# A selective scan in one TensorE-heavy kernel: decay factors written into PSUM, u made in place, and a new order of the work

## What is computed

```python
x = silu(conv(x) + conv_b)                    # (B, 512, 512 channels)
dt = softplus(dt_low @ W_dt + b_dt)
A = -exp(A_log)                               # 512 channels x 16 states
h = exp(dt_t[..., None] * A) * h + (dt_t * x_t)[..., None] * B_t[:, None, :]
y_t = sum over states of h * C_t
y = (y + x * D) * silu(z)
```

## Time and profile before

| what | value |
|---|---|
| median of 3 runs | 4347.93 us (4346.42 to 4351.42) |
| profiled execution: its time | 4355.29 us |
| its span, first to last instruction | 4353.5 us |
| TensorE / VectorE / ScalarE / GpSimd busy | 3935.7 / 3872.0 / 2366.9 / 1724.7 us |
| mean granted clock of TensorE | 0.968 of full speed |
| DMA engines | 73.7% busy, 753.5 MB |

### The profile page before, as it was taken

How to read it: one execution, slowest core, us unless ns; L and a number is a source line. 1 busy time by engine, 2 the same in 40 slices (tenths; PEclk the granted TensorE clock), 3 DMA queues, 4 the chain that set the end, 5 groups by cost and what they waited for, 6 DMA issues and landing times.

```text
span 4353.5 us, 55576 instructions
## 1 busy us (share of the span) xinstructions
PE 3935.7 (90%) x18933; PEld 2043.7 (47%) x18933; DVE 3872.0 (89%) x5708; ACT 2366.9 (54%) x4341; POOL 1724.7 (40%) x1295
## 2 busy tenths in 40 slices
PE   5878889999999999999999999998989999998898
PEld 3333444444545445454544545454444545544555
DVE  7699989898998989899898989989899899998753
ACT  2444455656555565555556465565545656564544
POOL 1254434443434435353343444444344344433410
PEclk9989999999999999899999999999899999999999
DMA  2699787878778787876787777788786888878511
GB/s 64 160 209 219 173 210 167 203 161 191 181 166 202 177 202 166 185 192 160 184 188 188 178 178 189 164 209 174 167 199 140 207 171 218 177 183 190 135 55 42
DMA packets 241440, 753.50 MB, mean 173 GB/s; under 512 B 37650, under 2 KB 132659, under 8 KB 171524
## 3 DMA queue, kind: packets, MB, share of 16 engines
q1 hardware_dynamic: 241156, 749.95, 73.7%
HBM read 647.30 MB, written 101.71 MB: 172 GB/s over the span
## 4 chain that ended last, share of the span: by engine, by line
DVE 40%; PE 33%; DMA 10%; issue 9%; ACT 6%; POOL 1%; SPq 1%; DVEq 0%; ACTq 0%; POOLq 0%
DVE state L1767 11%; DVE mt L1846 6%; DVE u L1762 4%; PE m L1249 4%; DMA state<-dtx_scratch 3%; PE m L1276 3%; PE pd L1477 2%; DMA decay<-dt_scratch 2%; PE y L1350 2%; DMA gz_scratch<-front 2%; DVE front L1701 2%; PE y L1338 2%; DVE front L1672 2%; DVE front L1676 2%; DVE front L1578 1%
## 5 line engine op out<-in xcount | busy, mean ns | idle before, releaser
L824 POOL TENSOR_TENSOR state<-state,bc 128x1024 f32<-128x1024 f32 x512 | 1270.4, 2482 | 1305.8 <-DVE u L1762 1287.1
L1767 DVE TENSOR_TENSOR_SCAN state<-decay,u 128x1024 f32<-128x1024 f32 x512 | 1166.8, 2279 | 6.4 <-ACT decay L1050 1.7
L1050 ACT ACTIVATE decay<-decay,a_neg 128x511 f32<-128x511 f32 x1024 | 674.9, 713 | 168.3 <-DMA decay<-dt_scratch 167.6
L1249 PE MATMUL m<-w_gu,hats_m 128*128 128x480 f32 x1472 | 680.5, 582 | 67.1 <-DVE front L1676 44.5
L1762 DVE TENSOR_TENSOR u<-state,bc 128x1024 f32<-128x1024 f32 x512 | 640.8, 1252 | 45.1 <-DMA state<-dtx_scratch 36.4
L1249 PEld LDWEIGHTS m<-w_gu,hats_m 128*128 128x128 f32 x1472 | 255.4, 192 | 334.5 <-issue 154.6
L805 POOL TENSOR_TENSOR front<-front,hsc_m 128x704 f32<-128x704 f32 x128 | 199.3, 1557 | 509.3 <-DVE front L1581 509.3
L1276 PE MATMUL m<-w_dn,front 128*128 128x256 f32 x1476 | 366.4, 390 | 14.1 <-ACT front L983 13.2
L1196 PE MATMUL y<-minus,zero 128*128 128x512 bf16 x1292 | 341.8, 389 | 2.1 <-ACT vec L904 2.1
L1338 PE MATMUL y<-state,sel 128*32 128x512 f32 x2048 | 280.6, 621 | 47.6 <-POOL state L824 47.3
L1276 PEld LDWEIGHTS m<-w_dn,front 128*128 128x128 f32 x1476 | 270.1, 191 | 103.8 <-ACT front L983 48.8
(11 more groups left out here) (396 smaller groups left out, 7278.3 us busy)
## 6 DMA issues: line engine op xcount, KB each, us to landing
decay<-dt_scratch SPq DMA_DIRECT2D x256, 1024.0 KB, 7.4
state<-dtx_scratch SPq DMA_DIRECT2D x256, 1024.0 KB, 11.5
qk_scratch_main<-shared SPq DMA_DIRECT2D x60, 384.0 KB, 4.3
shared<-qk_scratch_main SPq DMA_DIRECT2D x360, 64.0 KB
kh<-qk_scratch_main SPq DMA_DIRECT2D x360, 64.0 KB
xs_scratch<-front SPq DMA_DIRECT2D x16, 1024.0 KB, 9.5
dt_scratch<-front SPq DMA_DIRECT2D x256, 64.0 KB, 2.7
dtx_scratch<-hats_m SPq DMA_DIRECT2D x256, 64.0 KB, 5.0
```

The lines of the kernel that those rows point to most:

```text
L824: eng.tensor_tensor(st, st, bc[:, 1:2, :].to_broadcast([P, WIDE, L]), ALU.mult).then_inc(scan_pool.sem, scan_pool.step(f"c{r}{h}"))
L1050: ins = eng.activation(d, d, ACT.Exp, scale=a_neg[:, g:g + 1])
L1249: mm = eng.matmul(f.bank(r, f"gu{t}{p}")[:, 0:2 * width], norm.hat_t[:, k, t * P:(t + 1) * P], w_gu[:, k, 2 * lo:2 * (lo + width)], start= ...
L1767: eng.tensor_tensor_scan(st, decay[:, n % ND, h * WIDE * L:(h + 1) * WIDE * L], u[:, :], 0.0, ALU.mult, ALU.add).then_inc(scan_dve.sem, sc ...
```

## The change

The exponentials now go from the decay slot into a PSUM tensor `powers` of 1024 columns, the former `u`; its column 0 of both banks is set to 0 once by two one-column copies, and the 64 memsets of `dt` are gone. Each pair of exponentials waits for the scan before it. u is computed in place in the state's slot, one operation of 2048 columns a round, and the scan reads `powers` and the state and writes the state. The decay slot is free for the next load when its last exponentials are done. GpSimd's first product of a round waits for the first scan, its second for the next round's u. All five strings of `ORDER` are new. Two places of `ORDER` (the begin of VectorE's string), and then the rest, without the renaming of `u` to `powers` in a memset:

```diff
@@ -78,168 +78,165 @@
...
     "DVE":
-        "33333333333333330000000000000000000000000000000000000000000000000000333333333333333330000000000000000333333300000000000110000000"
...
+        "33333333333333330000000000000000000000000000000000000000000000000000333333333333333333300000000000000003333300000000000000010100"
...
@@ -366,12 +363,12 @@
-        u = ctx.enter_context(nc.psum_tensor("u", [P, WIDE * L], F32))
+        powers = ctx.enter_context(nc.psum_tensor("powers", [P, WIDE * L], F32))
-        U = [u[:, 0:L], u[:, L:2 * L]]
+        U = [powers[:, 0:L], powers[:, L:2 * L]]
@@ -503,11 +500,11 @@
         head_act = Steps(sem("head_act"), ["x0", "x1"] + [f"{n}{m}" for n, m in CONVS] + ["pj"]
                          + [f"{n}{c}" for b in (0, 2) for part in (("abs", "exp", "one"), ("ln",)) for c in (b, b + 1) for n in part] + [f"tanhz{m}" for m in range(C)])
         head_dve = Steps(sem("head_dve"), [n for w, m in CONVS for n in ((f"tap{m}1", f"tap{m}2", f"tap{m}3") if w == "conv" else (f"silu{m}",))]
-                         + [f"{n}{c}" for c in range(C) for n in ("rest", "log", "dt", "dtx", "zero")] + [f"siluz{m}" for m in range(C)])
+                         + [f"{n}{c}" for c in range(C) for n in ("rest", "log", "dt", "dtx")] + [f"siluz{m}" for m in range(C)])
         scan_pe = Steps(sem("scan_pe"), [n for r in range(ROUNDS) for n in ([f"skip{r // Q}"] if r % Q == 0 else []) + [f"sum{r}"]] + [f"o{t}" for t in range(T)])
         scan_act = Steps(sem("scan_act"), [f"decay{r}{h}" for r in range(ROUNDS) for h in range(PARTS)] + ["res0", "res1"])
         scan_dve = Steps(sem("scan_dve"), [n for r in range(ROUNDS)
-                                           for n in ([f"gate{r // Q - 1}"] if r >= Q and r % Q == 1 else []) + [f"{n}{r}{h}" for h in range(PARTS) for n in ("u", "scan")]]
+                                           for n in ([f"gate{r // Q - 1}"] if r >= Q and r % Q == 1 else []) + [f"u{r}"] + [f"scan{r}{h}" for h in range(PARTS)]]
                          + [f"gate{C - 1}"])
         scan_pool = Steps(sem("scan_pool"), [f"c{r}{h}" for r in range(ROUNDS) for h in range(PARTS)])
         CONVW = lambda tap, c: vec[:, tap * C + c:tap * C + c + 1]
@@ -643,7 +640,7 @@
                 eng.wait_ge(head_act.sem, head_act.after(i, "pj"))
                 eng.dma_start(bc_scratch[i], pj[RK + 1:, :]).then_inc(bc_saved, 16)
                 for c in range(C):
-                    for name, src, dst, done in (("zero", dt, dt_scratch, dt_saved), ("dtx", dtx_of(i), dtx_scratch, dtx_saved)):
+                    for name, src, dst, done in (("dtx", dt, dt_scratch, dt_saved), ("dtx", dtx_of(i), dtx_scratch, dtx_saved)):
                         for j in range(Q):
                             yield
                             if j == 0:
@@ -666,7 +663,7 @@
 
                 def load_bc(w):
                     if i and w == 0:
-                        eng.wait_ge(scan_dve.sem, scan_dve.after(i - 1, f"u{ROUNDS - 1}{PARTS - 1}"))
+                        eng.wait_ge(scan_dve.sem, scan_dve.after(i - 1, f"u{ROUNDS - 1}"))
                     if i and w == 1:
                         eng.wait_ge(scan_pool.sem, scan_pool.after(i - 1, f"c{ROUNDS - 1}{PARTS - 1}"))
                     eng.wait_ge(bc_saved, 16 * (i + 1))
@@ -683,7 +680,7 @@
                     n, c = ROUNDS * i + r, r // Q
                     yield
                     if n >= ND:
-                        eng.wait_ge(scan_dve.sem, scan_dve.after((n - ND) // ROUNDS, f"scan{(n - ND) % ROUNDS}{PARTS - 1}"))
+                        eng.wait_ge(scan_act.sem, scan_act.after((n - ND) // ROUNDS, f"decay{(n - ND) % ROUNDS}{PARTS - 1}"))
                     if r % Q == 0:
                         eng.wait_ge(dt_saved[c % 2], 64 * (2 * i + c // 2 + 1))
                         eng.wait_ge(dtx_saved[c % 2], 64 * (2 * i + c // 2 + 1))
@@ -819,8 +816,8 @@
                         st = state[:, n % NU, h * WIDE * L:(h + 1) * WIDE * L].rearrange("p (j l) -> p j l", j=WIDE)
                         if r == 0 and h == 0:
                             eng.wait_ge(bc_loaded[1], 16 * (i + 1))
-                        m = r * PARTS + h + 1
-                        eng.wait_ge(scan_dve.sem, scan_dve.after(i, f"u{m // PARTS}{m % PARTS}" if m < ROUNDS * PARTS else f"scan{r}{h}"))
+                        behind = h == PARTS - 1 and r < ROUNDS - 1
+                        eng.wait_ge(scan_dve.sem, scan_dve.after(i, f"u{r + 1}" if behind else f"scan{r}{h}"))
                         eng.tensor_tensor(st, st, bc[:, 1:2, :].to_broadcast([P, WIDE, L]), ALU.mult
                                           ).then_inc(scan_pool.sem, scan_pool.step(f"c{r}{h}"))
 
@@ -1045,9 +1042,14 @@
                         yield
                         if j == 0:
                             eng.wait_ge(decay_loaded[n % ND], 16 * (n // ND + 1))
-                        d = decay[:, n % ND, j * L + 1:(j + 1) * L]
+                        if n == 0 and j == 0:
+                            for bank in U:
+                                eng.activation(bank[:, 0:1], zero16[:, 0:1], ACT.Copy)
+                        if (n or j) and j % WIDE == 0:
+                            m = n * PARTS + j // WIDE - 1
+                            eng.wait_ge(scan_dve.sem, scan_dve.after(m // PARTS // ROUNDS, f"scan{m // PARTS % ROUNDS}{m % PARTS}"))
                         g = (r // Q * Q + j) * Q + r % Q
-                        ins = eng.activation(d, d, ACT.Exp, scale=a_neg[:, g:g + 1])
+                        ins = eng.activation(U[j % WIDE][:, 1:L], decay[:, n % ND, j * L + 1:(j + 1) * L], ACT.Exp, scale=a_neg[:, g:g + 1])
                         if j % WIDE == WIDE - 1:
                             ins.then_inc(scan_act.sem, scan_act.step(f"decay{r}{j // WIDE}"))
                 for b in range(2):
@@ -1725,9 +1727,6 @@
                     if c >= 2:
                         eng.wait_ge(dtx_saved[b], 64 * (2 * i + 1))
                     eng.tensor_tensor(dtx_of(i)[:, b, :], dt[:, b, :], xs[:, c, :], ALU.mult).then_inc(head_dve.sem, head_dve.step(f"dtx{c}"))
-                    yield
-                    eng.wait_ge(head_dve.sem, head_dve.after(i, f"dtx{c}"))
-                    eng.memset(dt[:, b, 0:1], 0.0).then_inc(head_dve.sem, head_dve.step(f"zero{c}"))
                 for m in range(C):
                     yield
                     eng.wait_ge(head_act.sem, head_act.after(i, f"tanhz{m}"))
@@ -1749,22 +1748,19 @@
                     if r >= Q and r % Q == 1:
                         yield
                         finish(r // Q - 1)
+                    yield
+                    if r == 0:
+                        eng.wait_ge(bc_loaded[0], 16 * (i + 1))
+                    eng.wait_ge(state_loaded[n % NU], 16 * (n // NU + 1))
+                    rows = state[:, n % NU, :].rearrange("p (j l) -> p j l", j=Q)
+                    eng.tensor_tensor(rows, rows, bc[:, 0:1, :].to_broadcast([P, Q, L]), ALU.mult).then_inc(scan_dve.sem, scan_dve.step(f"u{r}"))
                     for h in range(PARTS):
                         yield
                         st = state[:, n % NU, h * WIDE * L:(h + 1) * WIDE * L]
                         if h == 0:
-                            if r == 0:
-                                eng.wait_ge(bc_loaded[0], 16 * (i + 1))
-                            eng.wait_ge(state_loaded[n % NU], 16 * (n // NU + 1))
-                        if n or h:
-                            m = (n * PARTS + h - 1) // PARTS
-                            eng.wait_ge(scan_dve.sem, scan_dve.after(m // ROUNDS, f"scan{m % ROUNDS}{(h - 1) % PARTS}"))
-                        eng.tensor_tensor(u[:, :].rearrange("p (j l) -> p j l", j=WIDE), st.rearrange("p (j l) -> p j l", j=WIDE),
-                                          bc[:, 0:1, :].to_broadcast([P, WIDE, L]), ALU.mult).then_inc(scan_dve.sem, scan_dve.step(f"u{r}{h}"))
-                        yield
-                        eng.wait_ge(scan_dve.sem, scan_dve.after(i, f"u{r}{h}"))
+                            eng.wait_ge(scan_dve.sem, scan_dve.after(i, f"u{r}"))
                         eng.wait_ge(scan_act.sem, scan_act.after(i, f"decay{r}{h}"))
-                        eng.tensor_tensor_scan(st, decay[:, n % ND, h * WIDE * L:(h + 1) * WIDE * L], u[:, :], 0.0, ALU.mult, ALU.add
+                        eng.tensor_tensor_scan(st, powers[:, :], st, 0.0, ALU.mult, ALU.add
                                                ).then_inc(scan_dve.sem, scan_dve.step(f"scan{r}{h}"))
                 yield
                 finish(C - 1)
```

309 lines of the change are left out of this document (153 added, 156 removed).

## The result

| | before | changed |
|---|---|---|
| median | 4347.18 us (4 runs) | **4388.92 us** (4387.04 to 4392.70, 4 runs) |
| ratio, 95% interval | | 1.010 [1.0078, 1.0122] |
| profiled execution: time, span | 4355.29, 4353.5 us | 4387.04, 4384.9 us |

The change makes the kernel 41.7 us slower. The forecast was 4330, on the other side of no change.

The account below looks back on a forecast made before the run. VectorE was taken to bound the kernel, having the least slack. Terms -47 - 4 + 24 + 9 + 10 - 10 = -18 from the profiled 4355.3 us gave 4337.3, less 7.4 4330 us; range 4283 to 4393.

Parts of the forecast that it names:

- the term for GpSimd's C products, +10 us: VectorE operations with two SBUF inputs held while GpSimd's earlier-released product runs: +10 us, bounds 0 and 96.
- the added 96 us: Products' remaining time at VectorE's two-SBUF-input operations, 291 us before and 387 after; a tenth was taken as paid.
- u, -47: On VectorE, 512 operations of 1024 columns become 256 of 2048: -47 us, bounds 15 and 73 of gain.
- busy down by 50 to 60 us: Sign that the forecast is right: VectorE's busy time in the profile after falls by 50 to 60 us.
- Handing over the exponentials, +24 and +9: VectorE's scans waiting for ScalarE's exponentials: +24 us in 88 short first-to-second gaps, +9 us in the other 168.
- The decay slot, -10: Slot freed when its exponentials are done, so SyncE's loads go out earlier and u waits less: -10 us, bounds 0 and -36.
- The memsets, -4: The 64 memsets of column 0, 59 ns each, are dropped: -4 us.
- the case without loss: Rival "no handover loss": short gaps lie where VectorE was idle anyway; -61 us, 4287 us, chance 0.09.
- the exponentials' rival: VectorE waits before scans for exponentials, ScalarE working in order: +43, 4391 us, chance 0.26; decides from 51 us of waiting.
- The mean of L1727 far over 794: Sign of the port rival: VectorE's L1727 with a mean far over its 794 ns in the profile after.
- absorbed: Rival of no change: TensorE, chains over ScalarE to other threads and short gaps use up VectorE's gain; 4348 us, chance 0.20.
- that of the port: Rival: VectorE pays all of the added 96 us at GpSimd's products; 4416 us, chance 0.05.

Follow-up runs that it names:

- the two runs without products: GpSimd's C product cut to 2 columns of each row of 512, in both kernels: changed 4334.3 us, the one before 4321.5 us.
- the spaced pair: Quantiser's row maxima stored in groups of four with gaps, same arithmetic: kernel before 4325.4 us, changed kernel 4352.0 us.
- the pair of reductions: Quantiser's two small TENSOR_SCALARs replaced by one-element TENSOR_REDUCEs, factors left out: changed kernel 4355.9 us, kernel before 4326.5 us.
- the split run: Changed kernel with u as two operations of 1024 columns back to back at the same place: 4415.2 us.

## Why the prediction was wrong

**The failed step is the term for GpSimd's C products, +10 us.** It measured about 30 us, by the medians of the two runs without products (16 to 42 with what is uncertain in them), and VectorE's busy time alone took 35.7. Two things were wrong in it:

- It counted only operations with two SBUF inputs. About half of it or more (19 us by the spaced pair, 16 by the pair of reductions) is paid by TENSOR_SCALARs of 44 and 64 elements. Their rows stood in the trace of before: median 186 ns, longest 2086, mean 308. I had quoted such a spread for u and not looked for it elsewhere. The Trainium skill's row on SBUF interfaces ("GPSIMD Engine Reference") names the 2-port mode too; I quoted the half on two inputs.
- It scaled the added 96 us by the tenth that VectorE had paid so far. The 28 us behind this tenth were too few: without the products VectorE was busy 52.6 us less. And a share of an old, hand-laid order carries nothing over to a new release: the early release alone, in the old order, cost 261 us.

**u, -47**: 26 us by the split run, inside the bounds of 15 and 73, but 21 us short of the term. The size of 2300 ns was right (2294 forecast). The durations fell by 51.9 us, but half came back as lost overlap: 256 operations fewer by the 0.10 us of the earlier trace rows are 26. The sum held this in part; "busy down by 50 to 60 us" did not, and was wrong in itself: the durations of all of VectorE's operations add up to 19.2 us less (4220.7 to 4201.5), and what they overlap to 31.3 less (348.7 to 317.4), 0.10 us for each of the 320 instructions gone, which makes the 12.1 up.

**Handing over the exponentials, +24 and +9**: the wait is 70.8 us, twice the 33, and above the 51 from which the rival was to decide. It didn't decide: the dependence is worth 2 us with products and 14 without. A wait in the profile was taken for its price. The direction was right as far as can be told, the term too high, and the threshold of the rival was meaningless, since 59 us stay when nothing depends on a scan.

**The decay slot, -10**: the u waited 14.5 us for loads instead of 36.4, and SyncE 1211.7 instead of 1306.2. Right in kind; not priced by itself. **The memsets, -4**: 3.8 us of work gone, as said. The second product's later release was taken as 0 by the 47.3 us that TensorE waited for products; that wait is now 75.9.

**The range** was said to go from the case without loss to the price of the exponentials, which the prediction works out as 4287 and 4391; 4283 and 4393 don't follow from the sums. The measured 4388.9 lies near its upper end, where the exponentials' rival would put it (4391). That it comes so close is luck: that rival charges 94 us for waits whose cause is worth 2 to 14.

**The signs I named.** Right: the width of u, SyncE's wait. "The mean of L1727 far over 794" as the sign of the port stayed silent (763) while the port was the cause: I had chosen one operation, and the hold sits on whichever stands there. "Over 51 us at the scans" spoke for the wrong rival.

**What adds up and what doesn't.** -26 (u), -4 (memsets), +30 (products), +2 to +14 (dependence) make +2 to +14, and even with nothing for the loads 41.7 is not reached: some 28 to 40 us stay, or 16 if the products are given their upper 42. With products and dependence both out, the changed kernel (4319.8) only equals the one before (4321.5), though VectorE is busy 27 us less. The new order then has 62.9 us of waits at the scans. In the changed kernel L1720's wait for ScalarE is 61.7 us, where it was 35.5. So the rest most likely lies in how the threads wait for each other under an order that had to be new; no run shows it by itself. That the old one is worse for this program without the dependence (46 and 80 us) is shown; which waits hold the rest, and whether a better order has it, stays open. It would be the rival "absorbed", together with that of the port; I had set their prices apart and never added them.

## What to carry to other kernels

When a change moves the start of a long GpSimd operation, list every VectorE operation that can fall inside it, one-source operations within SBUF too, and look in the old trace for groups whose mean is far over their median: that is held time booked as work. Before paying for an exchange between engines, see whether the held operation can be laid out so that it isn't held; here gaps in a row of 44 numbers brought 18 us, and the whole redesign lost 42. And price a wait by taking its cause away, not by its length.

## What was not expected of the hardware

- A TENSOR_SCALAR on 128 x 44 or 64 float32 within SBUF, 0.19 us of work, takes up to 2.38 us beside a GpSimd product (L1569 of the changed kernel): it ends when the product ends (1005.26 against 1005.21; 40 to 53 ns behind the end in all 66 long cases), not a share of the way. The same values read as 11 or 17 groups of 4 take 0.20 to 0.22 us, with 201 ns the longest of 128 and 227 of 32.
- A TENSOR_REDUCE of the same values at the same place (193 ns) and the scan, whose second input was in PSUM before and whose first is now (2279 and 2280 ns), aren't held.
- ScalarE's exponentials of 511 columns are shorter when written to PSUM: 684 ns a piece against 713 when written in place in SBUF, and 714 in place under the new order.
- Releasing 256 products of 2.36 us at another time, with the same work on every engine, moved the end by 261 us in the kernel before and by 104 in the changed one.
- Among executions of one and the same kernel the time went with TensorE's mean granted clock: 4368.5 us at 0.965 and 4324.4 at 0.979. A variant compared at another clock carries this with it.
